# Two heads of cross-attention and the first tiles of the MLP behind it, in an interleaved order

## The reference

```python
def _cross_attention(q_in, kv_in, wq, bq, wk, bk, wv, bv, wo, bo, bias_k, bias_v):
    qh = (q_in @ wq + bq).reshape(b, q_len, H, K)        # 16 heads of 128
    kh = (kv_in @ wk + bk).reshape(b, t, H, K)
    vh = (kv_in @ wv + bv).reshape(b, t, H, K)
    kh = jnp.concatenate([kh, jnp.broadcast_to(bias_k, (b, 1, H, K))], axis=1)
    vh = jnp.concatenate([vh, jnp.broadcast_to(bias_v, (b, 1, H, K))], axis=1)
    logits = jnp.einsum('bqhk,bthk->bhqt', qh, kh) / scale
    weights = jax.nn.softmax(logits, axis=-1)
    ctx = jnp.einsum('bhqt,bthk->bqhk', weights, vh).reshape(b, q_len, H * K)
    return ctx @ wo + bo

x = x + _cross_attention(_layer_norm(x, ...), xf_1, ...)
x = x + _cross_attention(_layer_norm(x, ...), xf_2, ...)
h = _layer_norm(x, ln_mlp_scale, ln_mlp_offset)
x = x + jax.nn.gelu(h @ w_fc1 + b_fc1, approximate=False) @ w_fc2 + b_fc2
```

## Time and profile before

| | us |
|---|---|
| median of 3 runs | 1934.4 (1934.4 to 1938.42) |
| profiled execution, its own time | 1933.46 |
| its span | 1931.7 |
| PE busy | 1848.3 (96%) |
| DVE, ACT, POOL busy | 1112.1 (58%), 1045.8 (54%), 999.3 (52%) |
| mean granted clock of TensorE | 0.984 |
| chain that ended last | PE 85%, DVE 6%, issue 4%, POOL 3%, ACT 2% |

### The profile page before, as it was taken

One profiled execution on the slowest core, in us unless ns is written; L12 is line 12 of the kernel. 1 busy time (PEld: TensorE's weight loads), 2 busy tenths in 40 slices (PEclk: granted clock), 3 DMA queues, 4 the chain that ended last, 5 costly groups with the idle time before them and its releaser, 6 DMA issues.

```text
span 1931.7 us, 37703 instructions
## 1 busy us (share of the span) xinstructions
PE 1848.3 (96%) x14320; PEld 1503.4 (78%) x14320; DVE 1112.1 (58%) x2100; ACT 1045.8 (54%) x1949; POOL 999.3 (52%) x1140
## 2 busy tenths in 40 slices
PE   7999999889987999999999999999999998999999
PEld 5777789434454788888888888888888887977798
DVE  4656666489989455444444544544444445756574
ACT  4556553434443655665655656656666654346542
POOL 6777731476655444554544544545444534348530
PEclk9999999999998999999999999999999998999999
DMA  6000010000001213223222322322332220010000
GB/s 241 2 2 2 2 58 1 1 1 0 1 1 50 90 59 105 83 88 95 92 83 89 104 82 83 106 87 83 98 93 84 89 66 1 23 42 5 2 12 33
DMA packets 61841, 108.01 MB, mean 56 GB/s; under 512 B 7008, under 2 KB 42336, under 8 KB 60256
## 3 DMA queue, kind: packets, MB, share of 16 engines
q1 hardware_dynamic: 60784, 103.38, 17.0%
q10 hardware_dynamic: 880, 2.22, 0.3%
HBM read 103.47 MB, written 2.10 MB: 55 GB/s over the span
## 4 chain that ended last, share of the span: by engine, by line
PE 85%; DVE 6%; issue 4%; POOL 3%; ACT 2%; DMA 0%; DVEq 0%; SPq 0%; POOLq 0%; ACTq 0%
PE banks L864 18%; PE banks L935 9%; PE banks L892 9%; PE banks L646 7%; PE banks L629 7%; PE banks L471 7%; PE banks L924 6%; PE banks L905 3%; PE banks L480 3%; PE banks L553 2%; PE banks L528 2%; PE banks L539 2%; PE banks L510 2%; PE banks L465 2%; PE banks L913 1%
## 5 line engine op out<-in xcount | busy, mean ns | idle before, releaser
L1993 POOL TENSOR_TENSOR w_lo<-w2ring,w_hi 128x512 fp32r<-128x512 f32 x128 | 179.9, 1406 | 245.7 <-ACT w_hi L1138 245.7
L1815 DVE TENSOR_REDUCE nmax<-banks 128x4 f32<-128x260 f32 x128 | 54.2, 423 | 308.9 <-PE banks L905 308.9
L2076 POOL TENSOR_TENSOR wo_lo<-wo_ring,wo_hi 128x256 fp32r<-128x256 f32 x128 | 93.2, 737 | 249.1 <-ACT wo_hi L1346 249.0
L1803 DVE TENSOR_TENSOR v<-banks,dbv 128x512 f32<-128x512 f32 x128 | 88.5, 692 | 157.6 <-PE banks L892 157.5
L1346 ACT ACTIVATE wo_hi<-wo_ring 128x256 fp32r<-128x256 f32 x128 | 53.2, 417 | 188.9 <-PE banks L935 188.1
L935 PE MATMUL banks<-wo_hi,c_hi 128*128 128x256 f32 x512 | 148.5, 290 | 4.4 <-DVE c_lo L1808 4.4
L935 PE MATMUL banks<-wo_lo,c_hi 128*128 128x256 f32 x512 | 145.7, 285 | 0.0
L935 PE MATMUL banks<-wo_hi,c_lo 128*128 128x256 f32 x512 | 145.6, 284 | 0.0
L1333 ACT ACTIVATE k<-banks,cols 128x512 f32<-128x512 f32 x128 | 88.1, 689 | 80.5 <-PE banks L864 80.5
L924 PE MATMUL banks<-PT,v 128*128 128x128 f32 x1024 | 124.7, 275 | 1.0 <-issue 0.8
L924 PEld LDWEIGHTS banks<-PT,v 128*128 128x128 f32 x1024 | 119.7, 192 | 1.6 <-issue 1.2
(11 more groups left out here) (236 smaller groups left out, 5422.2 us busy)
## 6 DMA issues: line engine op xcount, KB each, us to landing
w2ring<-in_w SPq DMA_DIRECT2D x128, 384.0 KB, 3.2
b2ring<-in_b SPq DMA_DIRECT2D x128, 128.0 KB, 3.9
wo_ring<-in_wo SPq DMA_DIRECT2D x128, 128.0 KB, 3.2
mlp_w<-in_mlp SPq DMA_DIRECT2D x6, 1024.0 KB, 7.4
wl<-in_wres SPq DMA_DIRECT2D x1, 2688.0 KB, 8.6
X<-in_x_in SPq DMA_DIRECT2D x4, 512.0 KB, 11.5
wb<-in_wres SPq DMA_DIRECT2D x2, 1024.0 KB, 11.4
ctxT<-in_ctx_in SPq DMA_DIRECT2D x4, 512.0 KB, 19.1
```

The costliest lines, as they stand in the source:

```text
L1803: V.tensor_tensor(v2[i], held(("v2", v, i)).rearrange("p (s d) -> p s d", s=HV), dbv, ALU.add).then_inc(S["l2_v"], 1)
L1993: G.tensor_tensor(w2_lo[:, n % 2, :], w2ring[:, n % HR, 0:2 * KT * P], w2_hi[:, n % 2, :].bitcast(f32), ALU.subtract).then_inc(S["l2_wlo"], 1)
L2076: G.tensor_tensor(wo_lo[:, n % 2, :], wo_ring[:, n % WR, :], wo_hi[:, n % 2, :].bitcast(f32), ALU.subtract).then_inc(S["l2_wolo"], 1)
```

## The change

The loop over pairs ends on PE, ACT and POOL ahead of the turning of the last pair (PE breaks right behind its scores). The rest of the pair is moved behind `yield None`: projection of heads 124 and 125 and turning behind up tile 0, the weighing behind up tile 2, the projections of heads 126 and 127 behind up tiles 3 and 4 (with their down tiles). ACT, DVE and POOL get their steps at matching places. The splitting of the weights of the first up tiles is moved from the start of `mlp(1)` into the iteration of heads 124 and 125, and is of four tiles in place of two.

```diff
-LEAD = (4, 2, 4)
+LEAD = (4, 4, 4)
...
@@ PE, cross2, in the loop over pairs
                             for i in both:
                                 query(i + 2)
                                 keys(i + 2)
+                        else:
+
+                            break
...
                     yield None
+                    for i in both:
+                        project(i - 2)
+                    for i in both:
+                        turn(i)
+                    yield
+                    yield
+                    for i in both:
+                        weigh(i)
+                    yield
                     project(NH - 2)
                     yield
                     project(NH - 1)
...
@@ ACT, mlp
-                    if m == 1:
-                        for i in range(LEAD[m]):
-                            up_weights_hi(m, i)
...
@@ ACT, cross2
+                        if n + 2 == NH:
+                            break
...
+                        if n + 4 == NH:
+
+                            for i in range(LEAD[1]):
+                                act.wait_ge(S["l2_wlo"], NH - 2)
+                                act.wait_ge(S["l2_wvlo"], NH - 2)
+                                up_weights_hi(1, i)
                         yield 1
                     yield None
+                    for i in both:
+                        turned(i)
+                    for i in both:
+                        out_weights_hi(i)
+                    yield
+                    yield
+                    for i in both:
+                        context_hi(i)
                     yield
...
@@ POOL, mlp
-                    if m == 1:
-                        for i in range(LEAD[m]):
-                            up_weights_lo(m, i)
...
@@ POOL, cross2
+                        if n + 2 == NH:
+                            break
...
+                        if n + 4 == NH:
+                            for head in range(LEAD[1]):
+                                up_weights_lo(1, head)
                         yield 1
                     yield None
+                    for head in both:
+                        out_weights_lo(head)
                     yield
```

## The result

| | before | changed |
|---|---|---|
| median | 1934.4 us | 1923.86 us (5 runs, 1918.79 to 1924.17) |
| ratio | | 0.9935, 95% interval 0.9922 to 0.9949 |
| profiled execution | 1933.46 us | 1923.86 us |
| its span | 1931.7 us | 1922.0 us |
| mean granted clock | 0.984 | 0.987 |

The median fell by 10.5 us; 1923.0 was forecast, with 11.4 us. The ratio on record is not the quotient of the two medians, which is 0.9945. Its interval excludes no change, and by more than the 0.2% that the prediction took for what a measurement of this kernel can tell.

A forecast was written before the change was run, and what follows sets the result against it. The seam between layer 2 and the second MLP was taken as latency-bound, the rest as PE-bound. Up tile 5 at 1614.5 instead of 1626.21 gives 11.7 us, less 0.3 contention 11.4: 1923.0 us, range 1919.5 to 1929.0.

The forecast's parts named there:

- What bounds the piece: From the last scores to up tile 5: 15.0 of 33.65 us are waits or half clock, 10.0 in three gaps.
- Up tile 0: Behind the last scores on PE: starts 1.31 us behind the first weight copy, gap 1.0 us in place of 3.65.
- The cover: Up tile 0 and the old projection run unbroken on PE until the probabilities are ready, covering the 3.65 us gap.
- The new wait: Down tile 0 waits for banks 4 and 5 until DVE makes the low context parts: gap 2.3 us.
- POOL beside DVE: POOL's early splits run beside DVE's softmax: 0.3 us taken for late probabilities, capped at 0.9.
- The clock: Rival: clock drops once behind the gap ahead of down tile 0, costing 1.5 us; gain 9.9, 1924.5 us; chance 0.37.
- the pace: Rival: ACT or DVE runs late in the first MLP tiles, PE loses 3 to 6 us; 1926.0 to 1929.0; chance 0.07.
- The slower case: Norm's scale still comes at 1612.76, down tile 0 waits 12 us: 1935.4 us; slower if after 1615.7; chance 0.03.

The follow-up runs named there:

- The order alone: Changed kernel with the first four weight tiles split at the start of the MLP again, interleaved order kept: 1924.36 us, ratio 0.9956 to the kernel before.
- the three experiments: Changed kernel with ACT's norm behind gelu 3 (1923.46 us), with low context parts ahead of gelu part 2 on DVE (1924.11 us), and with both (1920.83 us).
- two tiles: Changed kernel with two weight tiles split beside heads 124 and 125 instead of four: 1923.12 us, ratio 0.9953 to the kernel before.
- split only: Kernel before, old order, with four weight tiles split beside heads 124 and 125: 1932.49 us, ratio 0.9998.

## Why the prediction was right

**What bounds the piece.** Right. 15.0 us of waits and half clock were to be had, and what was left, 3.6 us by the forecast, was 23.49 - 18.6 = 4.9. A fourth gap of 0.48 us, between the turnings of heads 126 and 127, was not among the three: it is part of the 5 us put down to the clock.

**Up tile 0.** Gap 1.0 forecast, 0.85 measured; PE gets going 1.30 us behind the first weight copy, as at the old place. The rows of another stage's start carried over. The difference lies in where the copy was put: in the rows the MLP's first copy starts 0.11 us ahead of the end of the context copy before it, and the prediction let the moved one start 0.02 behind it.

**The cover.** Right on every step that the profile shows. Up tile 1 starts 5.53 us behind the last scores, 5.7 by the forecast; the turning waits for nothing. The order alone makes 6.5 of the 10.2 us.

**The new wait.** Right in place and size: 2.3 forecast, 2.20 measured. Incomplete in its cause. The step "on ACT their high parts stand behind two gelus and the next norm" names one holder; gelu part 2 on DVE is the other, and the three experiments show that moving either alone gains nothing. What the prediction missed is the stretching beside POOL: the subtractions of gelu parts 1 and 2, of 0.69 us, took 1.25 and 1.10, and the cast of part 2, of 0.43, took 0.96. By an estimate from these rows, DVE would have been free at 1606.3 instead of 1607.70 without it, and ACT alone would have held the low part; no run tried that.

**POOL beside DVE.** The first probability took 0.66 instead of 0.42 us, and the turning did not feel it. So 0.3 us at that place was 0. The contention struck other steps than the one that I had priced with it, the gelu parts on DVE.
By the exclusive lock that the Trainium skill describes (SBUF — State Buffer, Who interferes with whom) DVE's operations with two SBUF inputs wait beside POOL; the rows agree, with 1.25 us for the gelu subtraction, and with 1.41 us, undisturbed, for two low context parts, one operand of which lies in PSUM. The cast has one input and was stretched as well, 0.96 us for 0.43; two inputs are not its reason.

**The clock.** Here the likeliest case was not the one that happened. I gave 0.50 to a gap without a drop and 0.37 to a drop with a price of 1.5 us; the drop came, at 1.75, and the gain of the piece is 10.16 against 9.9 in that rival. The step that was off is the price of nothing put on the gap in the forecast, because its size was "about the size at which rows disagree". Of the six profiles with a gap of 2.1 to 2.4 us in this piece, five fell to half behind it, with a granted clock of 0.52 to 0.54 in the 3.4 us that follow, and one kept its clock (two tiles; the row is in the last section). The Trainium skill has the clock fall after a whole idle stretch (TensorE: Matmul & The Clock Gate, The HAM clock gate), which would leave a short gap free; these profiles don't bear that out.

**The number.** 1923.86 lies 0.9 us from 1923.0, and that closeness is luck: the second median of the same program was 1921.11. The piece is the better judge, with 10.16 us against 11.4: 1.75 for the clock, less the 0.3 of contention that did not come and 0.2 in small terms. The upper end of the range, 1929.0, is said to take in the clock, 0.9 of contention and a loss of 6 us to the pace; together they give 1931.1, and 1929.0 is the pace alone.

**Rivals.** Another engine did not set the pace, with DVE busy 17.22 of 23.50 us and no gap on PE from up tile 5 on to 1640 us. The slower case fell with its condition: the norm's scale was ready 9.8 us behind the last scores (1604.46), where it was 20.2 us behind them before (1612.76).

## What to carry to other kernels

When a dependent chain at the end of a stage leaves PE idle, put the next stage's first independent tiles into it, and make their operands before the chain starts. Then look for the bank or buffer that the moved work now frees late: here the new wait and its half clock cost 3.95 of the 15.0 us that the old waits did, and one tile of distance closed it. A wait has one name in a trace and may have two holders; if moving the named one changes nothing, look at what the waiting engine was doing itself, and move both.

## What the runs showed of the hardware

A gap of about 2 us on PE can go either way for the clock. Behind 2.19 us ahead of up tile 3, in the two-tile kernel, it stayed whole:

```profile
1607.40:1612.00 4.60, 4.60 (x32) 4.22 (x33) 4.04 (x5) 2.90 (x7) 4.60 (x4) 1.00 0.01 2
```

and behind one of 3.1 us ahead of the first MLP, two profiles of the same program differ. The changed kernel, and its second profile:

```profile
236.60:246.80 10.20, 9.36 (x57) 8.06 (x58) 3.19 (x6) 3.18 (x5) 2.14 (x2) 0.50 0.00 0
```

```profile
233.00:246.00 13.00, 9.88 (x112) 8.33 (x111) 6.62 (x9) 6.43 (x9) 4.89 (x3) 1.00 0.01 2
```

The same step of PE (L553) starts at 232.17 and 231.32 us ahead of this gap, and at 247.66 and 242.52 behind it, so the slow stretch makes 4.3 of the 5.2 us by which the last scores end earlier in the second profile, 1589.48 against 1594.68; the spans are 1916.9 and 1922.0. Most of the rest is there from the start: the 48 first transposes end at 13.94 and 13.11 us. So stretches ahead of the piece, and not the piece, make the difference between these two profiles.

The same two places explain the 2.12 us that the changed kernel's profile is late at the start of the piece: before, the first transposes ended at 13.06 us instead of 13.94, and the slow stretch ahead of the first MLP was shorter, so that the step behind it starts at 245.61 instead of 247.66. The 1.66 us that it gains behind the piece are of this kind too. In the last layer, whose order is the same, the kernel before had a slow stretch of 6.8 us and the changed one of half that (PE's L646 ahead of it starts at 1817.55 and 1809.52, L553 behind it at 1826.61 and 1816.98, which is 1.6 us):

```profile
1818.30:1825.10 6.80, 6.80 (x53) 5.91 (x52) 1.59 (x5) 1.20 (x2) 1.90 (x1) 0.50 0.01 2
```

```profile
1810.20:1813.50 3.30, 3.30 (x35) 2.45 (x35) 0.99 (x3) 0.00 (x0) 1.90 (x1) 0.50 0.00 0
1813.60:1816.90 3.30, 3.30 (x28) 2.80 (x24) 0.68 (x2) 2.29 (x4) 0.00 (x0) 1.00 0.02 5
```

The length of a gap alone does not decide. In the last attention the changed and the two-tile kernel have the same gap of 1.97 us, and the clock stayed whole behind it in the first (1725.31) and fell in the second (1723.99):

```profile
1725.40:1729.00 3.60, 3.60 (x74) 3.10 (x75) 2.15 (x4) 1.87 (x3) 0.76 (x2) 1.00 0.91 350
```

```profile
1725.10:1731.80 6.70, 6.70 (x45) 4.63 (x45) 3.03 (x4) 1.69 (x2) 3.26 (x4) 0.50 0.67 276
```

What does decide is left open here.

The scatter hides what is done to a piece of 20 us: a change of 2.3 us in the piece (split only) could not be told in ten runs, while the piece itself repeats to 0.02 us.

DVE and POOL were both stretched where both worked from SBUF: the gelu parts on DVE took 1.25, 0.96 and 1.10 us for 0.69, 0.43 and 0.69, and two output weights on POOL 1.88 us for twice 0.73. The low context part, with one operand in PSUM, kept its 1.38 to 1.41 us for two in this piece of every profile, also while POOL was busy all through it (changed kernel, 1607.70 to 1609.11).
